# Moments of x1 by an accumulator and a ScalarE pass of squares; the last chunk of A h0 in two groups between the maps

## The chip, the cores and the metric

One core of one Trainium2 chip runs the whole program. The metric is the device time of one execution in microseconds (us). The engines are TensorE (PE, with its weight loads PEld), VectorE (DVE), ScalarE (ACT), GpSimd (POOL) and SyncE (SP, which here only issues DMAs). Each engine works through its own instructions in order and waits at semaphores.

## The reference, cut to what matters

Two graph layers over 1250 nodes with 512 features and 40000 edges.

```python
h0 = relu(layernorm(x))
msg = (h0[src] + edge_attr) @ Wm.T + bm                       # first layer
agg = segment_sum(msg, dst) / max(deg, 1)
out = h0 + gelu(concat(h0, agg) @ Wu.T + bu)
x1  = x + layernorm(out) * gamma + beta
h1  = relu(layernorm(x1))                                     # second layer
rst = (1 + eps) * h1 + segment_sum(h1[src], dst)
x2  = x1 + relu(rst @ W1 + b1) @ W2 + b2 + h1
```

## The kernel before, in words

Nodes lie in NT = 10 blocks of 128. A is the 1250 x 1250 matrix of edge counts, so that a sum over neighbours is a product with A. Up to about 251 us the kernel streams the edges, builds A and forms most of A h0. What is left of A h0 is the chunk of the last 226 nodes: ten `piece` steps on PE, each with eight matmuls, called in groups by `late` (L1292) between the maps.

The change lies in the stretch that follows, from 251 to about 331 us, in which the first layer ends and the second begins. Its order is written out by hand, one loop for each engine, with k as the step and b as the block:

- PE (L1296 to L1319): `map_agg(b)` multiplies block b's sums with the folded weights; `late` puts the ten pieces behind maps 2, 3, 4 and 5 as groups of 2, 3, 3 and 2; from b = 5 on `transpose_h1(b - 5)` and from b = 6 on `times_A(b - 6, "A")` follow each map, and after map 9 there are only transposes, `times_A` of chunk A and of chunk B as a filler. `map_agg(b)` waits for `update(b - 2)` of DVE, because it writes into the same PSUM bank. `transpose_h1(b)` waits for `h1(b)` of ACT.
- DVE (L997 to L1005): the list `STEPS` gives each piece of work with a lag; in step k it does `update(k)`, `center(k-2)`, `add_h0(k-1)`, `add_x(k-2)`, `o_moments(k-1)`, `shift(k-3)`, `x1_moments(k-2)`, `add_beta(k-1)`, `o_moments2(k-1)`, `x1_moments2(k-2)`, `o_variance(k-1)`, `x1_variance(k-2)` and `low_h1(k-4)`. `add_x(b)` writes x1 of block b to `U`; `x1_moments` and `x1_moments2` take its mean and variance with the two batch-norm instructions.
- ACT (L591 to L598): in step k a conversion `full_conv(k + 2)` of A, `gelu(k)`, `h0_again(k + 1)`, then `h1(k-3)`, `h1_high(k-3)` and `h1T(k-3)`. `h0_again(b)` makes h0 of a block again from a fresh copy of x in one of three buffers `xt`, and waits until that copy has landed.
- SP (`load_x`, L370): the copy of x for block b goes into `xt[b % 3]`, so from b = 3 on SP waits for `add_x(b - 3)`, the last reader of that buffer, before it issues the DMA.
- POOL (L429 to L436): the two powers of -1/2, `rs` for the first layer norm and `rs2` for that of x1.

`shift(b)` makes the bias of `h1(b)` from `rs2`, and `low_h1(b)` the low part of h1 that `times_A(b)` needs.

Of the kernel before, what the change touches and what calls it, by code (L numbers as in the profile page):

```python
# [5 lines left out]
F32 = mybir.dt.float32  # L6
# [4 lines left out]
ALU = mybir.AluOpType  # L11
# [3 lines left out]
P = 128  # L15
# [7 lines left out]
EPS = 1e-5  # L23
# [7 lines left out]
def gnn_kernel(nc, x, src, dst, edge, Wm, bm, Wu, bu, gamma, beta, W1, b1, W2, b2, eps, out):  # L31
# [54 lines left out]
    assert IN_LOOP <= 2 * NT and HAS_AT[-1] < NG and DEG_AT < OUT_AT and len(FOLD_AT) == HB - 1  # L86
    assert len(BIAS_AT) == NT and all(BIAS_AT[b] <= HAS_AT[b] for b in range(NT))
    DEG_BANK = 2
    CHUNK_BANK = [0, 1, 4, 5]

    at = [-(-nc.sbuf_base // 64) * 64]

    def place(name, shape, dt, offset=None):
        size = mybir.dt.size(dt)
        for n in shape[1:]:
            size *= n
        if offset is None:
            offset = at[0]
            at[0] += -(-size // 32) * 32
        return nc.alloc_sbuf_tensor_at(name, shape, dt, offset=offset), offset  # L100
# [91 lines left out]
    rs0, _ = place("rs0", [P, NT], F32)  # L192
    nb0, _ = place("nb0", [P, NT], F32)
    nb, _ = place("nb", [P, NT], F32)
    degs, _ = place("degs", [P, NT], F32)
    rdeg, _ = place("rdeg", [P, NT], F32)
    has, _ = place("has", [P, NT], F32)
    assert at[0] <= nc.sbuf_usable_end, at[0] - nc.sbuf_usable_end
# [2 lines left out]
    with ctx:  # L201
        ps = ctx.enter_context(nc.psum_tensor("ps", [P, 8, 512], F32))

        def sem(name):
            return ctx.enter_context(nc.semaphore(name))
# [95 lines left out]
        wu2_in = [sem(f"wu2_in{half}") for half in range(2)]  # L301
        wuT_done = sem("wuT_done")
        wuT_mm = sem("wuT_mm")
        x1_aggr = sem("x1_aggr")
        x1_ready = sem("x1_ready")
        x1_stats = sem("x1_stats")
        x_in = sem("x_in")
        xb_ready = sem("xb_ready")
        y_done = sem("y_done")
# [81 lines left out]
        @block.gpsimd  # L391
        def _(pool):
            nc.gpsimd.memset(dst_i[:], NP - 1).then_inc(pads_set, 1)
            nc.gpsimd.memset(src_i[:], 0).then_inc(pads_set, 1)
            nc.gpsimd.iota(iotaF[:], [[1, P]], base=0, channel_multiplier=0, allow_small_or_imprecise_dtypes=True).then_inc(consts, 1)
            nc.gpsimd.iota(pid[:], [[1, 1]], base=0, channel_multiplier=1, allow_small_or_imprecise_dtypes=True).then_inc(consts, 1)
            nc.gpsimd.memset(mhalf[:], -0.5).then_inc(consts, 1)
            nc.gpsimd.memset(onesF[:], 1.0).then_inc(consts, 1)
            nc.gpsimd.memset(offs[:], 0).then_inc(consts, 1)
            nc.gpsimd.memset(X[:, NT - 1, :], 0.0).then_inc(pads_set, 1)  # L400
            nc.gpsimd.iota(iotaP[:], [[1, 256], [0, 2]], base=0, channel_multiplier=0, allow_small_or_imprecise_dtypes=True).then_inc(consts, 1)

            pool.wait_ge(bm_in, 16)
            nc.gpsimd.tensor_copy(bmB[:], bmC[:].rearrange("p (m a) -> p m a", a=1).broadcast_to([P, FC, P])).then_inc(bmB_done, 1)

            pool.wait_ge(consts, 3)
            pool.wait_ge(ve_ready, 1)
            nc.gpsimd.tensor_tensor(rs0[:], ve[:], mhalf[:], ALU.pow).then_inc(rs_ready, 1)

            def add_sums_of(n):  # L410
                _, loaded = nc.values_load_multi_w_load_instructions(
                    offrow[0:1, n * 4:n * 4 + 2].bitcast(I32), engines=(mybir.EngineType.Pool,), min_val=0, max_val=(NP << 16) - 1,
                    skip_runtime_bounds_check_because="a pair of least indices of nodes")
                for half, first in enumerate((loaded[0] & 0xFFFF, loaded[0] >> 16)):
                    first = nc.s_assert_within(first, 0, NP - 1, skip_runtime_bounds_check_because="each is the least of indices of nodes")
                    cols = aggT[:, :, bass.ds(first, W)]
                    if half == 0:
                        pool.wait_ge(turned_out, n + 1)
                    if n > 0 or half > 0:
                        pool.wait_ge(early_step, n * 2 + half)  # L420
                    sums = turned_sums[n % TURNS][:].rearrange("p (f q) -> p f q", f=FC)[:, :, half * QUAD:half * QUAD + W]
                    nc.gpsimd.tensor_tensor(cols, sums, cols, ALU.add).then_inc(early_step, 1)  # L422

            pool.wait_ge(offs_in, 16)
            pool.wait_ge(sums_zero, 1)
            for n in range(EARLY):
                add_sums_of(n)

            for k in range(NT + 1):  # L429
                if k < NT:  # L430
                    pool.wait_ge(ve1_ready, k + 1)
                    nc.gpsimd.tensor_tensor(rs[:, k:k + 1], ve[:, k:k + 1], mhalf[:, 0:1], ALU.pow).then_inc(rs1_ready, 1)  # L432
                if k > 0:
                    b = k - 1
                    pool.wait_ge(ve2_ready, b + 1)
                    nc.gpsimd.tensor_tensor(rs2[:, b:b + 1], ve2[:, b:b + 1], mhalf[:, 0:1], ALU.pow).then_inc(rs2_ready, 1)  # L436

            pool.wait_ge(h1_ready, NT)
            pool.wait_ge(split1, NT)
            with pool.Fori(0, NT) as b:  # L440
                t = U[:, bass.ds(b, 1), :]
                nc.gpsimd.tensor_tensor(t, t, b2B[:].rearrange("p (a d) -> p a d", a=1), ALU.add).then_inc(res_step, 1)
                pool.wait_ge(res_step, b * 3 + 1)
                nc.gpsimd.tensor_tensor(t, t, Hh[:, bass.ds(b, 1), :].bitcast(F32), ALU.add).then_inc(res_step, 1)
                pool.wait_ge(res_step, b * 3 + 2)
                nc.gpsimd.tensor_tensor(t, t, Hl[:, bass.ds(b, 1), :].bitcast(F32), ALU.add).then_inc(res_step, 1)
# [3 lines left out]
        def _(act):  # L450
# [108 lines left out]
            def full_conv(c):  # L559
                nc.scalar.copy(AR[:, c, :], A16[:, c, 0:NP]).then_inc(conv, 1)  # L560
# [7 lines left out]
            def gelu(b):  # L568
                act.wait_ge(t_ready, b + 1)
                nc.scalar.activation(tt[b % TB][:], tt[b % TB][:], ACT.Gelu).then_inc(g_ready, 1)  # L570

            def h1(b):
                act.wait_ge(nb2_ready, b + 1)
                act.wait_ge(piece_mm, 2 * NT + b + 1)
                nc.scalar.activation(X[:, b, :], U[:, b, :], ACT.Relu, bias=nb[:, b:b + 1], scale=rs2[:, b:b + 1]).then_inc(h1_ready, 1)

            def h1_high(b):
# [9 lines left out]
            act.wait_ge(eps_ready, 2)  # L587
            full_conv(0)
            h0_again(0)
            full_conv(1)  # L590
            for k in range(NT + 4):  # L591
                if k + 2 < NT:
                    full_conv(k + 2)
                for work, lag in ((gelu, 0), (h1, 3), (h1_high, 3), (h1T, 3)):
                    if 0 <= k - lag < NT:
                        work(k - lag)
                    if work is gelu and k + 1 < NT:
                        h0_again(k + 1)  # L598
# [15 lines left out]
        def _(dve):  # L614
# [352 lines left out]
            def add_x(b):  # L967
                dve.wait_ge(centered, b + 1)
                dve.wait_ge(rs1_ready, b + 1)
                dve.wait_ge(xb_ready, b + 1)  # L970
                V.scalar_tensor_tensor(U[:, b, :], tt[b % TB][:], rs[:, b:b + 1], xt[b % TB][:], ALU.mult, ALU.add).then_inc(x1_ready, 1)

            def x1_moments(b):
                dve.wait_ge(x1_ready, b + 1)
                V.bn_stats(stats[:, b, :], U[:, b, :]).then_inc(x1_stats, 1)

            def x1_moments2(b):
                dve.wait_ge(x1_stats, b + 1)
                V.bn_aggr(mv2[:, b, :], stats[:, b, :]).then_inc(x1_aggr, 1)

            def x1_variance(b):
                dve.wait_ge(x1_aggr, b + 1)
                V.tensor_scalar(ve2[:, b:b + 1], mv2[:, b, 1:2], EPS, None, ALU.add).then_inc(ve2_ready, 1)

            def shift(b):
                dve.wait_ge(rs2_ready, b + 1)
                V.scalar_tensor_tensor(nb[:, b:b + 1], mv2[:, b, 0:1], -1.0, rs2[:, b:b + 1], ALU.mult, ALU.mult).then_inc(nb2_ready, 1)

            def low_h1(b):
                dve.wait_ge(hi1_ready, b + 1)  # L990
# [3 lines left out]
            dve.wait_ge(late_in, 48)  # L994
            dve.wait_ge(deg_step, 3 + NT)

            STEPS = [(update, 0), (center, 2), (add_h0, 1), (add_x, 2), (o_moments, 1), (shift, 3), (x1_moments, 2), (add_beta, 1), (o_moments2, 1),  # L997
                     (x1_moments2, 2), (o_variance, 1), (x1_variance, 2), (low_h1, 4)]
            for k in range(NT + 5):
                if k == 5:  # L1000
                    dve.wait_ge(piece_mm, 3 * NT)
# [27 lines left out]
        def _(pe):  # L1029
# [262 lines left out]
            def late(count):  # L1292
                for _ in range(count):
                    piece(late_pieces.pop(0))

            for b in range(5):  # L1296
                map_agg(b)
                late((0, 0, 2, 3, 3)[b])
            for b in range(5, NT):
                map_agg(b)  # L1300
                if b == 5:
                    late(2)
                    assert not late_pieces
                transpose_h1(b - 5)
                if b == 6:
                    pe.wait_ge(agg_done, 2 * FC + 1)
                if b > 5:
                    times_A(b - 6, "A")
# [74 lines left out]
```

## Time and profile before

| | us |
|---|---|
| median of 3 runs (489.90 to 492.35) | 490.38 |
| the profiled execution | 489.93 |
| its span | 488.1 |
| PE busy | 472.6 (97%) |
| DVE busy | 269.4 (55%) |
| ACT busy | 158.0 (32%) |
| POOL busy | 122.2 (25%) |

The profile is of one execution. The span runs from the first to the last instruction; 1.83 us of the execution's time lie outside it. In a timeline row the first number is the start in us from the span's start, the second the duration, then engine, line, operation, output and inputs, and in brackets the idle time before the row with what ended it. Instructions overlap by about 0.1 us on ACT and DVE, so what one costs its engine is read from start to start. The modelled end of a matmul lies up to 0.17 us behind the start of the next one.

### The profile page before, as it was taken

To read this page: it belongs to the slowest core of one execution; us is meant where nothing else is said; L and a number is where in the kernel's file an instruction comes from. 1 tells how busy PE (TensorE), PEld (TensorE's weight loads), DVE (VectorE), ACT (ScalarE), POOL (GpSimd) and SP (SyncE) were. 2 spreads that over 40 slices of the span, in tenths; PEclk is the share of its full clock that TensorE was granted. 3 is DMA by queue.
4 is the path that set the end of the run, shared out by engine and by line. 5 is a ranking of instruction groups with operands and counts; after the bars stand their busy time and mean duration, and the time that the engine had idled before them with its cause. 6 is when DMAs were issued, how large, how long until landed. Compare 5 with 4: busy or idle time off the path is not lost.

```text
span 488.1 us, 9290 instructions
## 1 busy us (share of the span) xinstructions
PE 472.6 (97%) x3275; PEld 277.4 (57%) x3275; DVE 269.4 (55%) x621; ACT 158.0 (32%) x291; POOL 122.2 (25%) x183
## 2 busy tenths in 40 slices
PE   4999999999999999999999999899999999999997
PEld 3545555555555446776766655699744449444442
DVE  4789878787878887977857699923000000011011
ACT  6726633332333327411047287620012123000000
POOL 4005433444343432000001113349990000000000
PEclk9899999999999999999999999999999999999999
DMA  8998999999999999999430111040130000010111
GB/s 297 381 351 282 410 389 395 398 407 401 396 391 397 397 401 405 401 339 299 147 109 24 43 30 53 0 173 1 45 128 1 0 0 1 21 43 21 44 43 38
DMA packets 31641, 98.92 MB, mean 203 GB/s; under 512 B 3593, under 2 KB 4617, under 8 KB 31595
## 3 DMA queue, kind: packets, MB, share of 16 engines
q1 hardware_dynamic: 30458, 97.27, 53.1%
q10 hardware_dynamic: 1136, 1.05, 0.7%
q8 instruction: 27, 0.44, 0.4%
q14 instruction: 20, 0.16, 0.1%
HBM read 95.76 MB, written 2.56 MB: 201 GB/s over the span
## 4 chain that ended last, share of the span: by engine, by line
PE 81%; DVE 10%; DMA 4%; issue 3%; SPq 1%; POOL 1%; DVEq 0%; POOLq 0%
PE ps L1355 14%; PE ps L1340 14%; PE ps L1091 10%; PE ps L1137 7%; PE ps L1110 6%; PE ps L1190 6%; PE ps L1191 5%; PE ps L1287 4%; PE ps L1099 4%; DMA X<-in_x_dram 4%; PE ps L1119 4%; PE ps L1263 3%; PE ps L1264 3%; DVE A L696 2%; DVE stats L777 1%
## 5 line engine op out<-in xcount | busy, mean ns | idle before, releaser
L422 POOL TENSOR_TENSOR aggT<-turned_sums,aggT 128x88 f32 x118 | 62.5, 530 | 88.1 <-ACT turned_sums L487 74.8
L1025 DVE TENSOR_TENSOR U<-ps,U 128x512 f32<-128x512 f32 (+1 forms) x10 | 6.9, 693 | 128.5 <-PE ps L1355 128.5
L696 DVE TENSOR_TENSOR A<-ps,A 128x220 f32 x158 | 60.7, 384 | 28.6 <-PE ps L1110 18.0
L1355 PE MATMUL ps<-W2s,hid 128*128 128x512 f32 (+1 forms) x160 | 68.8, 592 | 0.0
L1340 PE MATMUL ps<-aggT,W1s 128*128 (+1 forms) x192 | 67.3, 513 | 0.0
L1091 PE MATMUL ps<-ea,oneD 128*22 128x256 f32 x944 | 62.7, 383 | 0.0
L1340 PEld LDWEIGHTS ps<-aggT,W1s 128*128 128x128 f32 x192 | 36.4, 190 | 30.7 <-issue 30.6
L1355 PEld LDWEIGHTS ps<-W2s,hid 128*128 128x128 f32 (+1 forms) x160 | 30.0, 188 | 38.2 <-issue 38.2
L481 ACT COPY packed_sums<-ps 128x256 f32<-128x256 f32 x59 | 22.0, 372 | 90.4 <-PE ps L1091 90.4
L1091 PEld LDWEIGHTS ps<-ea,oneD 128*22 128x22 f32 x944 | 22.6, 101 | 46.5 <-issue 21.7
L1263 PE MATMUL ps<-AR,Hh 128*128 128x256 f32 (+2 forms) x160 | 44.0, 311 | 0.7 <-DVE Hl L992 0.7
L1264 PE MATMUL ps<-AR,Hl 128*128 128x256 f32 (+2 forms) x160 | 43.0, 306 | 0.0
L1110 PE MATMUL ps<-oneK,oneS 128*128 128x220 bf16 x316 | 41.2, 260 | 1.7 <-DVE A L696 1.5
L675 DVE TENSOR_TENSOR oneK<-iotaP,P_key 128x1760 bf16<-128x1760 bf16 (+1 forms) x40 | 42.3, 1057 | 0.0
L1137 PE MATMUL ps<-Wu1T,U 128*128 128x512 f32 x80 | 41.3, 598 | 0.0
L605 ACT ACTIVATE hid<-ps,b1C 128x512 f32 (+1 forms) x24 | 14.6, 608 | 77.7 <-PE ps L1340 77.7
L432 POOL TENSOR_TENSOR rs<-ve,mhalf 128x1 f32<-128x1 f32 x10 | 8.3, 829 | 113.1 <-DVE ve L957 113.1
L1287 PE MATMUL ps<-CT,aggT 128*128 128x512 f32 x80 | 35.7, 592 | 0.0
L1190 PE MATMUL ps<-ARc,Hh 128*128 128x512 f32 x80 | 33.8, 423 | 0.0
L1110 PEld LDWEIGHTS ps<-oneK,oneS 128*128 128x128 bf16 x316 | 29.7, 97 | 5.0 <-DVE oneK L675 2.2
L1263 PEld LDWEIGHTS ps<-AR,Hh 128*128 128x128 f32 x160 | 30.2, 189 | 2.7 <-DVE Hl L992 1.1
L1191 PE MATMUL ps<-ARc,Hl 128*128 128x512 f32 x80 | 31.6, 394 | 0.0
(133 smaller groups left out, 642.7 us busy)
## 6 DMA issues: line engine op xcount, KB each, us to landing
ea<-in_edge_attr_dram SPq DMA_DIRECT2D x78, 1024.0 KB, 7.8
X<-in_x_dram SPq DMA_DIRECT2D x1, 2304.0 KB
xt<-in_x_dram SPq DMA_DIRECT2D x9, 256.0 KB, 3.5
out_dram<-U SPq DMA_DIRECT2D x9, 256.0 KB
W1s<-in_L_gnn_W_dram SPq DMA_DIRECT2D x1, 2048.0 KB, 9.1
W2s<-in_L_gnn_W_dram SPq DMA_DIRECT2D x1, 2048.0 KB, 8.5
WuN<-in_L_gnn_Wu_dram ACTq DMA_DIRECT2D x2, 512.0 KB, 4.4
WuN<-in_L_gnn_Wu_dram SPq DMA_DIRECT2D x1, 1024.0 KB, 6.8
```

The lines of the kernel that those rows point to most:

```text
L422: nc.gpsimd.tensor_tensor(cols, sums, cols, ALU.add).then_inc(early_step, 1)
L696: V.tensor_tensor(cols, ps[:, 4 + m % 2, half * KW:(half + 1) * KW].rearrange("p (h w) -> p h w", w=W), cols, ALU.add).then_inc(add_step, 1)
L1091: last = T.matmul(to.rearrange("p (c d) -> p c d", c=2), oneD[h][:, g * 2 + j, :], data, start=j == 0, stop=j == 1)
L1110: last = T.matmul(ps[:, 4 + m % 2, (j // 2) * KW:(j // 2 + 1) * KW], sources[:, j // 2, :, j % 2], keys[:, j // 2, :, j % 2], start=j % 2 ...
L1137: quarter = T.matmul(ps[:, ASIDE_BANK["u1", b], :], U[:, b, f * P:(f + 1) * P], Wu1T[:, f, :], start=f == 0, stop=f == FC - 1)
L1190: T.matmul(to, Hh[:, c, rows], here, start=c == 0 and (q < 2 or f % 2 == 0), stop=False)
L1191: last = T.matmul(to, Hl[:, c, rows], here, start=False, stop=c == NT - 1 and (q < 2 or f % 2 == 1))
L1263: T.matmul(to, Hh[:, b, rows], AR[:, b, start:start + cols], start=b == 0 and (cols == 512 or f % 2 == 0), stop=False)
L1264: last = T.matmul(to, Hl[:, b, rows], AR[:, b, start:start + cols], start=False, stop=b == NT - 1 and (cols == 512 or f % 2 == 1))
L1287: last = T.matmul(ps[:, 2 + b % 2, :], aggT[:, f, b * P:(b + 1) * P], CT[:, f, :], start=f == 0, stop=f == FC - 1)
L1340: last = T.matmul(ps[:, CHUNK_BANK[k % 4], 0:cols], W1s[:, f, k * P:(k + 1) * P], aggT[:, f, bass.ds(start, cols)], start=f == 0, stop=f = ...
L1355: last = T.matmul(ps[0:rows, 6 + b % 2, :], hid[:, k, b * P:b * P + rows], W2s[:, k, :], start=k == 0, stop=k == KC - 1)
```

## The change

The two batch-norm instructions on x1 are replaced. `add_x` also writes the sum of its output row into `x1_sum` (laid over `degs`, which is no longer read by then). `x1_moments` becomes one [128 x 1] multiplication that makes minus the mean. A new ACT step `x1_squares` squares `U` plus that bias into `X` (which `h1` overwrites afterwards) and accumulates the sum of squares. `x1_variance` on DVE waits for that and moves from lag 2 near the end of a step to lag 3 at its head; `shift` moves behind `x1_moments`. On ACT `x1_squares(k-2)` stands behind `gelu(k)` and `h0_again(k+1)` and ahead of `h1(k-3)`. Two more conversions of A run before the ACT loop, whose own conversions begin at k = 2. POOL's loop takes `rs2(k-2)` ahead of `rs(k)`. On PE the ten pieces stand in two groups of five, behind map 1 and map 3.

```diff
+    CONV_AHEAD = 4
+    degs, degs_at = place("degs", [P, NT], F32)
+    x1_sum, _ = place("x1_sum", [P, NT], F32, degs_at)
...
-            for k in range(NT + 1):
+            for k in range(NT + 2):
+                if k >= 2:
+                    b = k - 2
+                    pool.wait_ge(ve2_ready, b + 1)
+                    nc.gpsimd.tensor_tensor(rs2[:, b:b + 1], ve2[:, b:b + 1], mhalf[:, 0:1], ALU.pow).then_inc(rs2_ready, 1)
                 if k < NT:
                     pool.wait_ge(ve1_ready, k + 1)
...
-                if k > 0:
-                    b = k - 1
-                    pool.wait_ge(ve2_ready, b + 1)
...
+            def x1_squares(b):
+                act.wait_ge(x1_mean, b + 1)
+                act.wait_ge(piece_mm, 2 * NT + b + 1)
+                nc.scalar.activation(X[:, b, :], U[:, b, :], ACT.Square, bias=mv2[:, b, 0:1], accum_out=mv2[:, b, 1:2]).then_inc(x1_square, 1)
...
-            full_conv(1)
+            for c in range(1, CONV_AHEAD):
+                full_conv(c)
             for k in range(NT + 4):
-                if k + 2 < NT:
-                    full_conv(k + 2)
-                for work, lag in ((gelu, 0), (h1, 3), (h1_high, 3), (h1T, 3)):
+                if k >= 2 and k - 2 + CONV_AHEAD < NT:
+                    full_conv(k - 2 + CONV_AHEAD)
+                for work, lag in ((gelu, 0), (x1_squares, 2), (h1, 3), (h1_high, 3), (h1T, 3)):
                     if 0 <= k - lag < NT:
                         work(k - lag)
                     if work is gelu and k + 1 < NT:
...
-                V.scalar_tensor_tensor(U[:, b, :], tt[b % TB][:], rs[:, b:b + 1], xt[b % TB][:], ALU.mult, ALU.add).then_inc(x1_ready, 1)
+                V.scalar_tensor_tensor(U[:, b, :], tt[b % TB][:], rs[:, b:b + 1], xt[b % TB][:], ALU.mult, ALU.add,
+                                       accum_out=x1_sum[:, b:b + 1]).then_inc(x1_ready, 1)
...
-                V.bn_stats(stats[:, b, :], U[:, b, :]).then_inc(x1_stats, 1)
-
-            def x1_moments2(b):
-                dve.wait_ge(x1_stats, b + 1)
-                V.bn_aggr(mv2[:, b, :], stats[:, b, :]).then_inc(x1_aggr, 1)
+                V.tensor_scalar(mv2[:, b, 0:1], x1_sum[:, b:b + 1], -1.0 / D, None, ALU.mult).then_inc(x1_mean, 1)
 
             def x1_variance(b):
-                dve.wait_ge(x1_aggr, b + 1)
-                V.tensor_scalar(ve2[:, b:b + 1], mv2[:, b, 1:2], EPS, None, ALU.add).then_inc(ve2_ready, 1)
+                dve.wait_ge(x1_square, b + 1)
+                V.tensor_scalar(ve2[:, b:b + 1], mv2[:, b, 1:2], 1.0 / D, EPS, ALU.mult, ALU.add).then_inc(ve2_ready, 1)
...
-            STEPS = [(update, 0), (center, 2), (add_h0, 1), (add_x, 2), (o_moments, 1), (shift, 3), (x1_moments, 2), (add_beta, 1), (o_moments2, 1),
-                     (x1_moments2, 2), (o_variance, 1), (x1_variance, 2), (low_h1, 4)]
+            STEPS = [(x1_variance, 3), (update, 0), (center, 2), (add_h0, 1), (add_x, 2), (o_moments, 1), (x1_moments, 2), (shift, 3), (add_beta, 1),
+                     (o_moments2, 1), (o_variance, 1), (low_h1, 4)]
...
-                late((0, 0, 2, 3, 3)[b])
+                late((0, 5, 0, 5, 0)[b])
...
-                if b == 5:
-                    late(2)
-                    assert not late_pieces
                 transpose_h1(b - 5)
```

## Rows read from the trace of the kernel before

**Rows 1.** Stretches: length, busy PE, PEld, DVE, ACT, POOL, granted clock, DMA share, GB/s.

```profile
12.00:14.00 2.00, 2.00 (x8) 1.41 (x7) 1.86 (x5) 1.17 (x2) 0.00 (x0) 0.50 1.01 403
280.00:325.00 45.00, 42.32 (x200) 29.67 (x199) 38.12 (x89) 30.52 (x43) 10.78 (x14) 1.00 0.21 69
290.00:305.00 15.00, 14.64 (x54) 8.80 (x53) 15.00 (x38) 10.91 (x17) 3.96 (x5) 1.00 0.18 50
```

**Rows 2.** Timeline of DVE, its step k = 8.

```profile
299.22 0.75 DVE L940 SCALAR_TENSOR_TENSOR tt<-ps,rdeg,U 128x512 f32<-128x512 f32 x1
...
300.54 0.68 DVE L945 TENSOR_TENSOR tt<-tt,h0t 128x512 f32<-128x512 f32 x1
301.14 0.74 DVE L971 SCALAR_TENSOR_TENSOR U<-tt,rs,xt 128x512 f32<-128x512 f32 x1
...
302.47 0.68 DVE L975 BATCH_NORM_STATS2 stats<-U 128x6 f32<-128x512 f32 x1
...
303.95 0.15 DVE L983 TENSOR_SCALAR ve<-mv 128x1 f32<-128x1 f32 x1
304.02 0.69 DVE L992 TENSOR_TENSOR Hl<-X,Hh 128x512 fp32r<-128x512 f32 x1
304.63 0.74 DVE L940 SCALAR_TENSOR_TENSOR tt<-ps,rdeg,U 128x512 f32<-128x512 f32 x1
```

**Rows 3.** Timeline of PE, maps 7 and 8, transposes of h1 of blocks 5 and 9.

```profile
287.51 3.60 PE L1287 MATMUL ps<-CT,aggT 128*128 128x512 f32 x8
...
293.25 3.60 PE L1287 MATMUL ps<-CT,aggT 128*128 128x512 f32 x8
...
306.35 0.63 PE L1272 MATMUL ps<-ident,X 128*128 128x128 f32 x4 [0.88 <-issue]
...
322.91 0.60 PE L1272 MATMUL ps<-ident,X 128*128 128x128 f32 x4
```

**Rows 4.** Timeline of PE, maps 0 to 4; last two rows DVE's, update(2), low_h1(0).

```profile
251.15 10.47 PE L1287 MATMUL ps<-CT,aggT 128*128 128x512 f32 x24
...
263.23 3.60 PE L1287 MATMUL ps<-CT,aggT 128*128 128x512 f32 x8
...
269.34 3.60 PE L1287 MATMUL ps<-CT,aggT 128*128 128x512 f32 x8
...
261.65 0.75 DVE L940 SCALAR_TENSOR_TENSOR tt<-ps,rdeg,U 128x512 f32<-128x512 f32 x1
...
281.39 0.69 DVE L992 TENSOR_TENSOR Hl<-X,Hh 128x512 fp32r<-128x512 f32 x1 [3.52 <-PE ps L1272]
```

**Rows 5.** Timelines of DVE and ACT: add_x (L971), h0_again (L566), h1 (L575).

```profile
263.58 0.74 DVE L971 SCALAR_TENSOR_TENSOR U<-tt,rs,xt 128x512 f32<-128x512 f32 x1
267.11 0.82 ACT L566 ACTIVATE h0t<-xt,nb,rs 128x512 f32<-128x512 f32 x1 [3.12 <-DMA xt<-in_x_dram]
...
268.80 0.75 DVE L971 SCALAR_TENSOR_TENSOR U<-tt,rs,xt 128x512 f32<-128x512 f32 x1
272.05 0.81 ACT L566 ACTIVATE h0t<-xt,nb,rs 128x512 f32<-128x512 f32 x1 [2.44 <-DMA xt<-in_x_dram]
272.77 0.80 ACT L575 ACTIVATE X<-U,nb,rs 128x512 f32<-128x512 f32 x1
...
290.33 0.74 DVE L971 SCALAR_TENSOR_TENSOR U<-tt,rs,xt 128x512 f32<-128x512 f32 x1
295.63 0.81 ACT L566 ACTIVATE h0t<-xt,nb,rs 128x512 f32<-128x512 f32 x1 [1.68 <-DMA xt<-in_x_dram]
```

**Rows 6.** Groups of ACT by line and shape: busy us, mean ns | idle before.

```profile
L566 ACT ACTIVATE h0t<-xt,nb,rs 128x512 f32<-128x512 f32 x10 | 8.1, 808 | 7.5 <-DMA xt<-in_x_dram 7.5
...
L570 ACT ACTIVATE tt<-tt 128x512 f32<-128x512 f32 x10 | 6.3, 626 | 0.0
...
L546 ACT ACT_TABLE_LOAD x1 | 1.3, 1283 | 0.0
L546 ACT ACTIVATE warm<-onesF 128x1 f32<-128x1 f32 x1 | 0.2, 203 | 0.0
```

More of the change, by code:

```diff
@@ L194, in gnn_kernel @@
     nb, _ = place("nb", [P, NT], F32)
-    degs, _ = place("degs", [P, NT], F32)
+    degs, degs_at = place("degs", [P, NT], F32)
+    x1_sum, _ = place("x1_sum", [P, NT], F32, degs_at)
     rdeg, _ = place("rdeg", [P, NT], F32)
@@ L303, in gnn_kernel @@
         wuT_mm = sem("wuT_mm")
-        x1_aggr = sem("x1_aggr")
+        x1_mean = sem("x1_mean")
         x1_ready = sem("x1_ready")
-        x1_stats = sem("x1_stats")
+        x1_square = sem("x1_square")
         x_in = sem("x_in")
@@ L432, in _ @@
                     nc.gpsimd.tensor_tensor(rs[:, k:k + 1], ve[:, k:k + 1], mhalf[:, 0:1], ALU.pow).then_inc(rs1_ready, 1)
-                if k > 0:
-                    b = k - 1
-                    pool.wait_ge(ve2_ready, b + 1)
-                    nc.gpsimd.tensor_tensor(rs2[:, b:b + 1], ve2[:, b:b + 1], mhalf[:, 0:1], ALU.pow).then_inc(rs2_ready, 1)
             pool.wait_ge(h1_ready, NT)
@@ L570, in gelu @@
                 nc.scalar.activation(tt[b % TB][:], tt[b % TB][:], ACT.Gelu).then_inc(g_ready, 1)
+            def x1_squares(b):
+                act.wait_ge(x1_mean, b + 1)
+                act.wait_ge(piece_mm, 2 * NT + b + 1)
+                nc.scalar.activation(X[:, b, :], U[:, b, :], ACT.Square, bias=mv2[:, b, 0:1], accum_out=mv2[:, b, 1:2]).then_inc(x1_square, 1)
             def h1(b):
                 act.wait_ge(nb2_ready, b + 1)
-                act.wait_ge(piece_mm, 2 * NT + b + 1)
+                act.wait_ge(x1_square, b + 1)
                 nc.scalar.activation(X[:, b, :], U[:, b, :], ACT.Relu, bias=nb[:, b:b + 1], scale=rs2[:, b:b + 1]).then_inc(h1_ready, 1)
@@ L970, in add_x @@
                 dve.wait_ge(xb_ready, b + 1)
-                V.scalar_tensor_tensor(U[:, b, :], tt[b % TB][:], rs[:, b:b + 1], xt[b % TB][:], ALU.mult, ALU.add).then_inc(x1_ready, 1)
+                V.scalar_tensor_tensor(U[:, b, :], tt[b % TB][:], rs[:, b:b + 1], xt[b % TB][:], ALU.mult, ALU.add,
+                                       accum_out=x1_sum[:, b:b + 1]).then_inc(x1_ready, 1)
             def x1_moments(b):
                 dve.wait_ge(x1_ready, b + 1)
-                V.bn_stats(stats[:, b, :], U[:, b, :]).then_inc(x1_stats, 1)
-            def x1_moments2(b):
-                dve.wait_ge(x1_stats, b + 1)
-                V.bn_aggr(mv2[:, b, :], stats[:, b, :]).then_inc(x1_aggr, 1)
+                V.tensor_scalar(mv2[:, b, 0:1], x1_sum[:, b:b + 1], -1.0 / D, None, ALU.mult).then_inc(x1_mean, 1)
             def x1_variance(b):
-                dve.wait_ge(x1_aggr, b + 1)
-                V.tensor_scalar(ve2[:, b:b + 1], mv2[:, b, 1:2], EPS, None, ALU.add).then_inc(ve2_ready, 1)
+                dve.wait_ge(x1_square, b + 1)
+                V.tensor_scalar(ve2[:, b:b + 1], mv2[:, b, 1:2], 1.0 / D, EPS, ALU.mult, ALU.add).then_inc(ve2_ready, 1)
             def shift(b):
                 dve.wait_ge(rs2_ready, b + 1)
-                V.scalar_tensor_tensor(nb[:, b:b + 1], mv2[:, b, 0:1], -1.0, rs2[:, b:b + 1], ALU.mult, ALU.mult).then_inc(nb2_ready, 1)
+                V.tensor_tensor(nb[:, b:b + 1], mv2[:, b, 0:1], rs2[:, b:b + 1], ALU.mult).then_inc(nb2_ready, 1)
             def low_h1(b):
```

## The prediction

> **What bounds the kernel now.** I read the stretches first, then DVE's and ACT's timelines between 251 and 331 us, then PE's. PE is the bound of the whole, and the stretch that the change touches is no exception: from 280 to 325 us PE is busy 42.32 of 45 us [rows 1], so it waits for 2.68 us in all. Those waits, and up to about 1 us more that the modelled ends of the matmuls before them hide, are all that a shorter DVE could give back. Inside that stretch DVE sets the pace: from 290 to 305 us it is busy 15.00 of 15.00 us, ACT 10.91 [rows 1]. One DVE step lasts 299.22 to 304.63 = 5.41 us [rows 2]. What PE does in a step there (a map, the transposes of a block, a block of chunk A) is 287.51 to 293.25 = 5.74 us with no wait inside [rows 3]. So DVE and PE run almost in step, and PE's waits stand at the transposes, as before block 5 at 306.35 [rows 3].
>
> **What the change takes off DVE.** Each step loses the batch-norm statistics of x1, 0.61 us from start to start with 0.68 busy [rows 2], and a small aggregate; it gains a [128 x 1] multiplication, about 0.07 by x1_variance's 303.95 to 304.02 [rows 2]. That alone would make the DVE step some 4.9 us, under PE's. How much of it counts depends on the new order of waits.
>
> **The new wait.** x1_variance(b) now stands at the head of DVE's step b+3 and waits for x1_squares(b) of ACT's step b+2. Behind that wait in DVE's queue stand update, center, add_h0 and add_x, the whole step. On ACT x1_squares(b) stands behind h0_again(b+3), which waits for the copy of x of block b+3 to land. SP issues that copy only once add_x(b) has released the buffer. So there is a closed round: x1_variance(b), update(b+3), center(b+1), add_h0(b+2), add_x(b+1), load of block b+4, h0_again(b+4), x1_squares(b+1), x1_variance(b+1). Before, the same late load only made ACT wait (7.5 us in four places [rows 6]); DVE did not ask ACT for anything that lay behind it until a step later.
>
> **One round, from rows.** x1_variance to the next instruction 0.07; update and center 299.22 to 300.54, 1.32; add_h0 300.54 to 301.14, 0.60; add_x 0.74 to its end [rows 2]. Then the load: from add_x's end to h0_again's start it took 267.11 - 264.32 = 2.79, 272.05 - 269.55 = 2.50 and once 295.63 - 291.07 = 4.56 us [rows 5]. Seven blocks load this way; I take the mean of the two near ones, 2.65, and one slow load in seven, (4.56 - 2.65) / 7 = 0.27: 2.9. h0_again to the next ACT instruction 272.05 to 272.77 = 0.72 [rows 5].
>
> Two prices have no row. **x1_squares:** gelu, with no pointer operand, takes 0.626 and h0_again, with two, 0.808 [rows 6]; with its one I take 0.72. Writing out the accumulator may be a further small instruction: nothing at least, 0.40 at most (two of the 128 x 1 activation of 0.203 [rows 6]); I take one, 0.20, since that is the smallest ACT instruction there is. Together 0.92, bounds 0.63 and 1.21. **The accumulator of add_x:** nothing at least, 0.20 at most in the plain case; I take 0.07, the issue of a [128 x 1] DVE instruction [rows 2]. Below nothing is excluded for both: the instructions do all that they did before, or are new.
>
> Sum: 0.07 + 1.32 + 0.60 + 0.81 + 2.9 + 0.72 + 0.92 = 7.34 us a round, against 5.41 on DVE and 5.74 on PE. ACT's own work does not reach that: 10.91 / 15 x 5.41 = 3.9 a step plus 0.92.
>
> A rule of the Trainium skill speaks against the accumulator: Vector Engine (DVE) Microarchitecture Reference, section "Points that are easy to get wrong", says that a scalar-tensor-tensor with two SBUF sources that are not bf16 runs at half throughput. add_x is one such already, without an accumulator, and takes 0.74 against add_h0's 0.68 [rows 2], so the trace does not show it; by the page each round would be longer, which is a rival below.
>
> **The two groups of pieces.** On PE nothing is won or lost by grouping: a map is 3.43 (three end after 10.47 and one lasts 3.60, so (10.47 - 3.60) / 2), a map and three pieces take 263.23 to 269.34 = 6.11 [rows 4], so a piece costs (6.11 - 3.43) / 3 = 0.89 with its change of weights in it. But all five of the first group now stand ahead of map 2, where none stood. update(2) waits for map 2, so it moves from 261.65 [rows 4] by 5 x 0.89 = 4.47 to 266.12. In the kernel before, DVE had room for that: it waited 3.52 us at low_h1(0), 281.39 [rows 4]. Now the rounds start there.
>
> **The other moves.** The two conversions ahead of the ACT loop cost nothing: ACT then waits for update(2) and the first load, as it did for 3.12 us before 267.11 [rows 5]. POOL's new order puts rs2 first, as DVE asks for it; shift has five DVE instructions of cover behind x1_variance. SP's queue: the load of W1, behind the last copy of x, waits for the last add_x and moves with it; what needs it moves as well. POOL's residual adds, which wait for the last h1, do the same.
>
> **The sum.** update(2) at 266.12; add_x(0) ends 1.32 + 0.60 + 0.81 = 2.73 later, 268.85; load, 271.75; h0_again, 272.47; x1_squares(0) done at 273.39. Six rounds of 7.34, 44.04, bring x1_squares(6) to 317.43; it is the last that stands behind a load (block 9). h1(5) follows on ACT, 0.80 [rows 5], and its transpose starts at 318.3 with a handover of 0.1. Before it started at 306.35 [rows 3]: 12.0 later. From there to the transpose of block 9 took 16.56 [rows 3], nearly all PE's work; it stays, give or take 0.5. PE's waits inside the rounds (7.34 - 5.74 = 1.6 each, and a long one where map 9 is done and update(9) is not) are this same time seen from PE, not a further cost. So the profiled execution goes from 489.93 to 501.9. The median of the runs lies 0.45 above that execution; 490.38 + 12.0 = **502.4**.
>
> Low end: load 2.50, squares 0.63, no price for add_x: 6.58 a round, 0.76 less in seven passes (the first pass and six rounds), -5.3: 497.1. High end: load 2.79 with two slow ones of seven, 3.30, squares 1.21, add_x 0.20: 8.16 a round, +0.82 x 7 = 5.7: 508.1.
>
> **Rivals.**
> - *DVE's gain counts (faster).* If x1_squares never waited behind a load, the pace would be PE's 5.74, and PE's waits of 2.68 and the 1 hidden behind modelled ends would go: 486.7. It decides where the round falls under 5.74: all terms but the load make 4.44, so the load must take under 1.3 us from add_x's end. The shortest in the trace is 2.50. For it: the chain of work that DVE carries is truly shorter, and one DVE-bound stretch is the only one with PE waits. 0.05.
> - *The load is hidden, but so is the gain (same).* With the load covered, update(2) still comes 4.47 late against a room of 3.52 [rows 4], about 1 us lost at the first transposes, and the rest a draw: 491.4. 0.07.
> - *The accumulating add_x passes at half rate (slower still).* Its issue, 0.66 by the update and center before it, doubles; some 0.6 x 7 = 4.2 more: 506.6. DVE is then not relieved at all, and the change does not do what it says. Against it is add_x's 0.74 today. 0.08.
> - *Square needs another table than Gelu.* Table loads are two in the whole trace, of 1.283 each, the last ahead of the first Gelu [rows 6], though Copy, Relu and Gelu alternate; if Square were not in the same table, x1_squares would carry one inside the round and gelu one outside: at least 1.28 x 7 = 9 more, 511. The Trainium skill, ScalarE: Activation LUTs, section "Table sets: the hidden batching unit", names relu, copy, identity and abs as present in every set and does not name square there; by its price of about 2.7 us for a switch (an estimate from that page) it would be some 19 more. 0.03.
> - *The clock.* PE runs at 1.00 throughout this stretch; early in the trace it was granted 0.50 at 12 to 14 us [rows 1], behind PE's idle start. With waits of 1.6 in each round and some 5 us before the transpose of block 5 it may fall again; at half rate a stretch like that one costs 1 to 3 us beyond what the rounds' own room covers: 503 to 505. 0.07.
>
> **How the numbers follow.** The forecast has 0.70, the rivals what stands behind them. The range is 497 to 508: it takes in the bounds of the unknown costs, the clock and the half rate, and leaves out the two cases without a loss, the table loads and a little at both ends, some 2 in 10. A measurement of this kernel can tell about 0.5% (2.5 us) from no change. Faster 0.05, same 0.07, slower 0.88.
>
> **What would show it.** Right: in the timeline of DVE after, x1_variance idles about 2.3 us in each of steps 4 to 9 and its releaser is ACT's Square; ACT's h0_again idles before almost each block, released by the DMA; the distance between two x1_variance is 7 to 7.5; the transpose of block 5 starts near 318, and all that follows keeps its length. Wrong: h0_again without idle time, DVE steps near 5, or PE without waits between 285 and 318. Accumulator and squares are read off directly: 0.74 to 0.81 for add_x, 0.7 to 0.9 for Square with its read. What would make it wrong altogether is a load that lands a good deal sooner than 2.5 us after add_x.

## The result and the profile after

The changed kernel takes 499.99 us (median of 5 runs, 499.79 to 502.46) against 490.38 for the kernel before: a ratio of 1.0189, 95% interval 1.0163 to 1.0214, 9.6 us slower. The forecast was 502.4, in a range of 497 to 508.

The profiled execution of the changed kernel took 502.46 us, the longest of its five; 2.87 us of what it has over that of before lie ahead of the first map (254.02 in place of 251.15 [rows 4]), where the two programs are the same. About half of this came up between 190 and 222 us, a stretch in which the granted clock fell to 0.50 for some 3 us and that of before did not. The stretch in question is therefore compared from its own first map on. From there to the transpose of block 9 it was 322.91 - 251.15 = 71.76 us before [rows 3, 4]; after it is 335.47 - 254.02 = 81.45, that is 9.69 more, as much as the medians lie apart. The timeline of PE after, first map and the transposes of blocks 1, 5, 6 and 9:

```profile
254.02 7.03 PE L1292 MATMUL ps<-CT,aggT 128*128 128x512 f32 x16
...
290.36 0.66 PE L1277 MATMUL ps<-ident,X 128*128 128x128 f32 x4 [2.77 <-ACT X L582]
...
318.16 1.11 PE L1277 MATMUL ps<-ident,X 128*128 128x128 f32 x4 [4.40 <-DVE tt L948]
323.99 0.60 PE L1277 MATMUL ps<-ident,X 128*128 128x128 f32 x4
...
335.47 0.60 PE L1277 MATMUL ps<-ident,X 128*128 128x128 f32 x4
```

PE now waits 2.77 us for block 1 and 4.40 us for block 5, where the row of before has 0.88 [rows 3]. The wait at block 5 ends with update(9): in both programs PE waits for the last update once, ahead of the transposes of blocks 5 to 9 (`pe.wait_ge(t_ready, NT)`). What lies behind it stands in the chain of work that ended last, here from one load of x to the next (start, duration, what):

```profile
278.63 2.57 DMA xt<-in_x_dram
281.36 0.58 issue
281.94 0.81 ACT X L577 x2
282.94 0.56 issue
283.50 0.74 DVE tt L969
284.25 0.60 DVE tt L953
284.84 0.68 DVE U L979 x2
285.55 2.51 DMA xt<-in_x_dram
```

This is the closed round, link by link: the load, h0_again (in the first "issue" piece), x1_squares on ACT (L577), x1_variance and update (in and just ahead of the second "issue" piece), center (L969), add_h0 (L953), add_x (L979), and the next load, which that add_x released. The chain repeats it seven times, and the load is its largest piece. The same round on DVE and on ACT, one step of each:

```profile
275.85 0.15 DVE L988 TENSOR_SCALAR ve<-mv 128x1 f32<-128x1 f32 x1 [2.65 <-ACT X L577]
275.92 0.74 DVE L948 SCALAR_TENSOR_TENSOR tt<-ps,rdeg,U 128x512 f32<-128x512 f32 x1
...
277.85 0.75 DVE L979 SCALAR_TENSOR_TENSOR U<-tt,rs,xt 128x512 f32<-128x512 f32 x1
278.52 0.08 DVE L979 DVE_READ_ACCUMULATOR U<-tt,rs,xt 128x1 f32 x1
278.52 0.69 DVE L957 BATCH_NORM_STATS2 stats<-tt 128x6 f32<-128x512 f32 x1
...
282.77 0.15 DVE L988 TENSOR_SCALAR ve<-mv 128x1 f32<-128x1 f32 x1 [2.57 <-ACT X L577]
...
317.29 0.15 DVE L988 TENSOR_SCALAR ve<-mv 128x1 f32<-128x1 f32 x1 [1.81 <-ACT X L577]
317.36 0.74 DVE L948 SCALAR_TENSOR_TENSOR tt<-ps,rdeg,U 128x512 f32<-128x512 f32 x1
```

```profile
281.22 0.81 ACT L568 ACTIVATE h0t<-xt,nb,rs 128x512 f32<-128x512 f32 x1 [3.72 <-DMA xt<-in_x_dram]
281.94 0.71 ACT L577 ACTIVATE X<-U,mv 128x512 f32<-128x512 f32 x1
282.55 0.19 ACT L577 ACTIVATION_READ_ACCUMULATOR X<-U,mv 128x1 f32 x1
...
317.17 0.80 ACT L582 ACTIVATE X<-U,nb,rs 128x512 f32<-128x512 f32 x1
```

x1_variance (L988) waits 2.65 and 2.57 us at the head of its step, for ACT; ACT's h0_again has just waited 3.72 for the load. The last row of each is update(9) and h1(5) (L582). Six rounds last 317.29 - 275.85 = 41.44 us, 6.91 each, against a step of 5.41 before [rows 2].

### The profile page after: what moved, and what is told of

It reads as the page before. It is cut to its first block, busy times and chain, and to the rows that moved or that the text cites. A ratio compares the mean times of both kernels' runs of the same rounds, so it can differ in the third digit from the quotient of the medians.

```text
span 500.7 us, 9320 instructions
## 1 busy us (share of the span) xinstructions
PE 476.4 (95%) x3275; PEld 280.2 (56%) x3275; DVE 264.0 (53%) x621; ACT 165.4 (33%) x311; POOL 121.5 (24%) x183
## 4 chain that ended last, share of the span: by engine, by line
PE 78%; DMA 7%; DVE 7%; issue 4%; ACT 1%; SPq 1%; DVEq 1%; POOL 0%; ACTq 0%; POOLq 0%
PE ps L1357 14%; PE ps L1342 13%; PE ps L1096 10%; PE ps L1142 7%; PE ps L1115 5%; PE ps L1195 5%; PE ps L1196 4%; PE ps L1268 4%; PE ps L1269 4%; DMA X<-in_x_dram 4%; PE ps L1104 4%; DMA xt<-in_x_dram 4%; PE ps L1124 4%; PE ps L1292 2%; DVE A L704 2%
## 5 line engine op out<-in xcount | busy, mean ns | idle before, releaser
L1268 PE MATMUL ps<-AR,Hh 128*128 128x256 f32 (+2 forms) x160 | 45.4, 319 | 0.0
L1269 PE MATMUL ps<-AR,Hl 128*128 128x256 f32 (+2 forms) x160 | 44.4, 313 | 0.0
L1268 PEld LDWEIGHTS ps<-AR,Hh 128*128 128x128 f32 x160 | 31.3, 196 | 1.8
```

The costliest lines, as they stand in the source:

```text
L1268: T.matmul(to, Hh[:, b, rows], AR[:, b, start:start + cols], start=b == 0 and (cols == 512 or f % 2 == 0), stop=False)
L1269: last = T.matmul(to, Hl[:, b, rows], AR[:, b, start:start + cols], start=False, stop=b == NT - 1 and (cols == 512 or f % 2 == 1))
```

## The experiments

All are compared with the kernel before on the same chip; the ratio is the kernel's time over that of the kernel before. "Transpose 5" and "stretch" are read from the one profile of each run, in us: from the first map to the transpose of block 5, and to that of block 9. The theory: the round through the load sets the pace. The rivals: the ScalarE pass and DVE's wait for it cost the time whatever stands ahead of them; the two groups of pieces cost it; the clock does.

| kernel | ratio, 95% interval | transpose 5 | stretch |
|---|---|---|---|
| before | | 55.20 | 71.76 |
| changed | 1.0189 (1.0163 to 1.0214) | 64.14 | 81.45 |
| squares ahead of h0_again | 1.0017 (0.9995 to 1.0040) | 56.81 | 72.40 |
| four buffers for x | 1.0042 (1.0027 to 1.0058) | 56.44 | 73.13 |
| wait behind add_x | 0.9977 (0.9956 to 0.9999) | 56.03 | 70.92 |
| four groups again | 1.0132 (1.0098 to 1.0166) | 62.52 | 79.20 |
| groups alone, on before | 1.0025 (1.0010 to 1.0040) | 55.63 | 72.62 |
| load in four parts | 1.0285 (1.0266 to 1.0304) | 68.10 | 85.58 |
| PE kept busy | 1.0192 (1.0173 to 1.0211) | 63.98 | 80.67 |
| open round | 0.9942 (0.9927 to 0.9957) | 53.54 | 68.82 |
| its order alone, on before | 1.0025 (1.0006 to 1.0044) | 55.63 | 72.07 |
| open round, two groups | 0.9951 (0.9933 to 0.9969) | 53.55 | 68.82 |

**The squares ahead of the load.** One line of ACT's order in the changed kernel:

```diff
-                    if work is gelu and k + 1 < NT:
+                    if work is x1_squares and k + 1 < NT:
                         h0_again(k + 1)
```

> The changed kernel with one edit: on ACT x1_squares(k-2) runs ahead of h0_again(k+1) instead of behind it, so no load stands between add_x(b) and x1_squares(b). Theory (the closed round through the load sets the pace, 6.91 us in the profile after): x1_variance to x1_variance falls to PE's 5.7, PE loses only its first transposes, and the time is 491 to 492 us. Rival 1 (the added pass on ACT and the wait of DVE for it cost the time, whatever stands ahead): the pass still lies on the way to h1 and DVE still waits for it at the head of its step, so the time stays at 498 to 500. Rival 2 (the two groups of pieces cost it): stays at 500.

Measured: 492.01 us, ratio 1.0017. The groups of ACT and DVE in its stretch (busy us, mean ns | idle before):

```profile
L568 ACT ACTIVATE h0t<-xt,nb,rs 128x512 f32<-128x512 f32 x10 | 8.1, 810 | 3.4 <-DMA xt<-in_x_dram 3.4
L988 DVE TENSOR_SCALAR ve<-mv 128x1 f32<-128x1 f32 x10 | 1.5, 151 | 3.2 <-ACT X L577 3.1
```

In the changed kernel the same two groups read:

```profile
L568 ACT ACTIVATE h0t<-xt,nb,rs 128x512 f32<-128x512 f32 x10 | 8.1, 810 | 16.6 <-DMA xt<-in_x_dram 16.6
L988 DVE TENSOR_SCALAR ve<-mv 128x1 f32<-128x1 f32 x10 | 1.5, 153 | 14.3 <-ACT X L577 14.3
```

x1_variance waits 3.2 us in all where the changed kernel has 14.3, with the same pass on ACT and the same wait at the head of DVE's step. Of the 9.69 us in the stretch, 9.05 are gone.

**The load a round earlier.** A fourth buffer, with all orders kept:

```diff
+    XB = 4
-    xt = [... w1_at + i * 2048)[0] for i in range(TB)]
+    xt = [... w1_at + i * 2048)[0] for i in range(XB)]
...
-                if b >= TB:
-                    sp.wait_ge(x1_ready, b - TB + 1)
+                if b >= XB:
+                    sp.wait_ge(x1_ready, b - XB + 1)
...
```

> The changed kernel with four buffers for the copies of x instead of three (the fourth lies in room that is free by then), all orders as in the changed kernel: the load for block b waits for add_x(b-4) instead of add_x(b-3), so it is issued one round earlier. Theory: h0_again no longer waits for a landing, the round loses the 2.6 us of the load and PE's 5.7 sets the pace; 491.5 to 492.5 us, a little over the kernel with the squares ahead, since h0_again's 0.72 stays in the round. Rival 1 (the added ACT pass and DVE's wait): 498 to 500. Rival 2 (groups): 500.

Measured: 492.91 us, ratio 1.0042. In the groups of ACT the wait for the load is gone, and it was the load alone that was moved; x1_variance still waits 3.8 us in all, for the pass on ACT:

```profile
L569 ACT ACTIVATE h0t<-xt,nb,rs 128x512 f32<-128x512 f32 x10 | 8.1, 806 | 0.0
L989 DVE TENSOR_SCALAR ve<-mv 128x1 f32<-128x1 f32 x10 | 1.5, 152 | 3.8 <-ACT X L578 3.8
```

**The wait elsewhere in DVE's queue.** `(x1_variance, 3)` behind `(add_x, 2)`, `(shift, 3)` behind `(add_beta, 1)`:

```diff
-            STEPS = [(x1_variance, 3), (update, 0), (center, 2), (add_h0, 1), (add_x, 2), (o_moments, 1), (x1_moments, 2), (shift, 3), (add_beta, 1),
+            STEPS = [(update, 0), (center, 2), (add_h0, 1), (add_x, 2), (x1_variance, 3), (o_moments, 1), (x1_moments, 2), (add_beta, 1), (shift, 3),
...
```

> The changed kernel with x1_variance moved in DVE's step from the head to behind add_x (shift goes behind add_beta); ACT's order, the buffers and the groups stay. Theory: what is wrong is what is queued behind the wait: add_x(b+1) no longer waits for x1_squares(b), so the load of block b+4 is released early and the round is open although each load still stands ahead of its squares; 489 to 491 us. Rival 1 (the pass itself is what costs): x1_squares ends no earlier against its add_x than now, 4.2 us behind it, and h1 waits for it as now, so 497 to 500.

Measured: 490.56 us, ratio 0.9977, so not slower than before at all. Each load still stands ahead of its squares; what changed is that add_x no longer queues behind the wait:

```profile
L988 DVE TENSOR_SCALAR ve<-mv 128x1 f32<-128x1 f32 x10 | 1.5, 152 | 0.1
L568 ACT ACTIVATE h0t<-xt,nb,rs 128x512 f32<-128x512 f32 x10 | 8.1, 806 | 4.8 <-DMA xt<-in_x_dram 4.8
```

So three different links, each opened by itself, give back nearly all. The first rival would have kept 497 us or more in each; it falls.

**More load.** The same bytes as four DMAs of 32 rows:

```diff
-                sp.dma_start(xt[b % TB][0:rows, :], x[b * P:b * P + rows, :]).then_inc(xt_in[b % TB], 16)
+                for n in range(4):
+                    part = slice(n * 32, min(rows, n * 32 + 32))
+                    sp.dma_start(xt[b % TB][part, :], x[b * P + part.start:b * P + part.stop, :]).then_inc(xt_in[b % TB], 16)
...
-                act.wait_ge(xt_in[b % TB], 16 * (b // TB + 1))
+                act.wait_ge(xt_in[b % TB], 64 * (b // TB + 1))
```

> The changed kernel with each load of x issued as four DMAs of 32 rows in place of one: same bytes, but the last is issued about 3 x 0.33 = 1 us later on SP's queue. Theory (every load lies in the round, in seven passes): each wait of h0_again ends about 1 us later, round 7.9 in place of 6.9, and the time grows by some 7 us, to 505 to 508. Rival 1 (the ACT pass, not the load, sets the round): the same 500 as the changed kernel, since ACT idles 1.5 us ahead of h0_again anyway.

Measured: 504.92 us, ratio 1.0285, just under what was expected, because a load came later by 0.6 and not by 1 us: h0_again starts 3.28 us behind the end of add_x in its third step, 274.12 - 270.84, where the changed kernel has 2.65 (274.30 - 271.65). Seven loads by 0.6 make 4.2; the stretch is 85.58 - 81.45 = 4.13 longer. Both engines of the round, ACT and DVE, have idle time in every step of this kernel, and still every 0.6 us of load is paid in full.

```profile
270.09 0.75 DVE L981 SCALAR_TENSOR_TENSOR U<-tt,rs,xt 128x512 f32<-128x512 f32 x1
...
274.12 0.81 ACT L570 ACTIVATE h0t<-xt,nb,rs 128x512 f32<-128x512 f32 x1 [4.54 <-DMA xt<-in_x_dram]
281.58 0.81 ACT L570 ACTIVATE h0t<-xt,nb,rs 128x512 f32<-128x512 f32 x1 [4.27 <-DMA xt<-in_x_dram]
```

**The groups.** First the changed kernel with `late((0, 0, 2, 3, 3)[b])` and `late(2)` behind map 5 again:

> The changed kernel with the ten pieces back in their four groups (2, 3, 3, 2 behind maps 2 to 5); the new moments stay. Theory: the rounds start earlier by at most the 4.47 us that map 2 no longer waits, less what PE's own first transpose, which cannot come sooner, holds them up: 1.5 to 2.5 us faster than the changed kernel, 497.5 to 498.5. Rival 2 (the groups are what costs): 490 to 491.

Measured: 497.79 us, ratio 1.0132; the stretch 2.25 us shorter than the changed kernel's. Then the kernel before with `late((0, 5, 0, 5, 0)[b])` alone:

> The kernel before with only the regrouping of the ten pieces (five behind map 1, five behind map 3); moments by the batch-norm instructions as before. Theory: on PE the grouping itself is free; DVE starts its steps 4.47 us later at update(2) and has 3.5 us of room, so about 0.9 us is lost at the transpose of block 1 and not won back: ratio 1.002 (491.3 us). Rival (the groups carry a good part of the loss): 494 or more. If the old version was right to have no room elsewhere, below 490.

Measured: ratio 1.0025, the stretch 0.86 longer, as large as expected but not where it was expected. Block 1's transpose lies 34.00 us behind the first map, as before (33.99); it is update(5) that starts 286.27 - 253.54 = 32.73 behind it where it was 283.01 - 251.15 = 31.86, and DVE, with steps of 5.4 us, carries these 0.87 us on until PE waits for update(9), ahead of the transpose of block 5:

```profile
286.27 0.74 DVE L940 SCALAR_TENSOR_TENSOR tt<-ps,rdeg,U 128x512 f32<-128x512 f32 x1
...
309.17 0.63 PE L1272 MATMUL ps<-ident,X 128*128 128x128 f32 x4 [1.89 <-DVE tt L940]
```

Of the 0.86 us, 0.43 stand at that transpose (55.63 against 55.20 in the table). The other 0.43 lie behind it, where the granted clock also fell, to 0.66 on average from 310 to 315 us; how much of this half is the clock's is open. So the groups cost up to 0.9 us by themselves, and 2.25 beside the closed round, whose start they delay. They are not what cost the 9.6.

**The clock.** In the changed kernel the granted clock falls at the 4.40 us wait: in stretches of half a microsecond it is 0.50, the lower of its two levels (1.2 and 2.4 GHz), from 317.0 to 323.5 us. In stretches of 5 us (length, PE busy, granted clock, DMA share, GB/s):

```profile
315.00:320.00 5.00, 1.84 (x7) 0.69 0.03 11
320.00:325.00 5.00, 5.00 (x22) 0.63 0.00 0
```

The edit puts matmuls into that wait, whose results the next transposes overwrite:

```diff
+    DUMMY = 16
...
+            pe.wait_ge(h1T_done, 4)
+            for n in range(DUMMY):
+                T.matmul(ps[:, 7, :], Hh[:, 0, 0:P], AR[:, 0, 0:512], start=n == 0, stop=n == DUMMY - 1)
             pe.wait_ge(t_ready, NT)
```

> The changed kernel with 16 extra matmuls of 128 x 512 on PE where it waits some 4.4 us for update(9) (their results are overwritten by the transposes that follow). In the profile after, PE's granted clock is 0.69 and 0.63 in the 10 us behind that wait, and the transposes of blocks 5 and 6 lie 5.83 us apart against 3.24 before. Theory: the clock falls because of that idle time; with PE kept busy it stays at 1.00, the two transposes lie 4.3 apart as the rounds of DVE and ACT ask, and the time is 0.5 to 1.5 us under the changed kernel's 500, the rest being hidden. Rival: the extra matmuls come on top and the time is 500 or more, the clock the same.

Measured: 500.35 us, ratio 1.0192, no different from the changed kernel's: the gain of 0.5 to 1.5 us that was expected did not show. Where it was meant to, the clock stayed at 1.00 in the one execution that was profiled, and the transposes of blocks 5 and 6 lie 321.82 - 317.68 = 4.14 us apart in place of 5.83. But in this execution it fell elsewhere, behind the wait for block 1, and without cost there, since the rounds have room:

```profile
290.00:295.00 5.00, 4.87 (x13) 0.50 0.17 52
...
320.00:325.00 5.00, 4.30 (x29) 1.00 0.00 0
```

Between the transposes of blocks 5 and 9 this kernel takes 334.37 - 317.68 = 16.69 us, the changed one 17.31, the kernel before 16.56 [rows 3]. The kernel with four buffers, whose clock stayed at 1.00 there, takes 16.69 as well (73.13 - 56.44). So the clock's fall costs about 0.6 us of the changed kernel's stretch, an estimate from one execution of each, and too little to be seen in the times of this run.

**A version that opens the round.** In DVE's step x1_variance stands behind center, shift behind add_x, low_h1 behind o_moments; ACT's order is gelu, h1, x1_squares, h1_high, h0_again, h1T; four groups.

```diff
-            STEPS = [(x1_variance, 3), (update, 0), (center, 2), (add_h0, 1), ...
+            STEPS = [(update, 0), (center, 2), (x1_variance, 3), (add_h0, 1), (add_x, 2), (shift, 3), (o_moments, 1), (low_h1, 4), (x1_moments, 2),
+                     (o_moments2, 1), (add_beta, 1), (o_variance, 1)]
...
-                for work, lag in ((gelu, 0), (x1_squares, 2), (h1, 3), (h1_high, 3), (h1T, 3)):
+                for work, lag in ((gelu, 0), (h1, 3), (x1_squares, 2), (h1_high, 3), (h1T, 3)):
...
-                    if work is gelu and k + 1 < NT:
+                    if work is h1_high and k + 1 < NT:
...
```

> The changed kernel's moments (accumulator and ScalarE pass) in an order with no closed round: in DVE's step x1_variance behind center, shift behind add_x, low_h1 behind o_moments; on ACT gelu, h1, x1_squares, h1_high, h0_again, h1T; the four old groups of pieces. Theory: PE's waits between blocks 1 and 5 go (0.6, 0.5 and 1.05 us), and with the later ones in part too: 2 to 2.8 us of the 3.6 that PE lost there, ratio 0.994 to 0.996 against the kernel before (487.8 to 488.5). Rival 1 (the pass on ACT costs time of its own): no better than the kernel before, 490 or more.

Measured: 487.67 us, ratio 0.9942 (0.9927 to 0.9957): faster than both kernels, by 2.9 us against before on the same chip (490.55). DVE's step is 4.9 us, and PE's wait for update(9) shrinks to 0.45:

```profile
288.98 0.74 DVE L948 SCALAR_TENSOR_TENSOR tt<-ps,rdeg,U 128x512 f32<-128x512 f32 x1
...
293.87 0.74 DVE L948 SCALAR_TENSOR_TENSOR tt<-ps,rdeg,U 128x512 f32<-128x512 f32 x1
...
305.13 0.66 PE L1277 MATMUL ps<-ident,X 128*128 128x128 f32 x4 [0.45 <-DVE tt L948]
```

Whether the order or the moments won this was asked with the same order in the kernel before (h0_again behind h1_high, shift behind add_x, low_h1 behind o_moments; batch-norm moments as before):

> The kernel before, its moments by the batch-norm instructions and its four groups kept, with only the order of the open-round version: in DVE's step shift behind add_x, low_h1 behind o_moments, and on ACT h0_again behind h1_high. Theory: what the open-round version won (ratio 0.9942) is the DVE time that the new moments free; with the batch-norm instructions DVE's step stays 5.4 us and the order alone wins nothing: 490 to 491.5 us, ratio 0.999 to 1.003. Rival: the order was the gain, and the moments did nothing: 487.5 to 488.5, ratio 0.994 to 0.996.

Measured: ratio 1.0025; the order alone wins nothing, and the interval lies above 1. Its steps on DVE are still 5.37 us (290.29 to 295.66), and PE waits 2.54 us for update(9):

```profile
290.29 0.74 DVE L940 SCALAR_TENSOR_TENSOR tt<-ps,rdeg,U 128x512 f32<-128x512 f32 x1
...
295.66 0.74 DVE L940 SCALAR_TENSOR_TENSOR tt<-ps,rdeg,U 128x512 f32<-128x512 f32 x1
...
307.19 0.66 PE L1272 MATMUL ps<-ident,X 128*128 128x128 f32 x4 [2.54 <-DVE tt L940]
```

Last, the open round with the two groups of five:

> The open-round version with the two groups of five in place of the four. Theory: the 0.9 us that the groups cost the kernel before came of DVE's small room behind a later update(2); with a DVE step near 4.9 us the room is there, and the groups cost nothing: 487.5 to 488.5 us, ratio 0.994 to 0.996, the same as with four groups. Rival: the groups cost their 0.9 us (ratio 1.0025 alone) whatever DVE does: 488.5 to 489.5, ratio 0.9965.

Measured: ratio 0.9951, and a stretch of 68.82, the same to the hundredth as with four groups. The interval alone (0.9933 to 0.9969) would not exclude the rival's 0.9965; the equal stretches speak for the theory, that a DVE with room pays nothing for a later update(2).

## Why the prediction was right

- **What bounds.** Right. PE's waits in the stretch were the ceiling of a gain: the open round took 2.94 us off the stretch (71.76 to 68.82), of the 2.68 and about 1 more that the prediction counted. DVE's step is 4.89 us there, where the prediction had some 4.9.
- **The new wait and the round.** Right in every link of the round; the chain of work names them in the order in which the prediction did. The link behind it was another: PE's transpose of block 5 was released by update(9), which ended at 318.10, and not by h1(5), which had ended at 317.97. Both come straight behind x1_squares(6), 0.13 us apart, so the sum hardly changes.
- **The signs.** h0_again waits for the DMA ahead of all seven blocks. x1_variance waits 2.65, 2.57, 0.88, 1.93, 2.21, 1.83 and 1.81 us for x1_squares, mean 1.98 in place of about 2.3, and two of them lie 6.91 apart on average and not 7 to 7.5. That the transpose of block 5 started at 318.16, "near 318", and that the profiled execution took 502.46 where 501.9 was forecast, is luck: this execution reached its first map 2.87 us later than that of before. Counted from there the transpose came at 64.14 and not at 318.3 - 251.15 = 67.15.
- **The size of the round.** 7.34 was forecast, 6.91 came. The load was the term taken too large: from add_x's end to h0_again it took 2.65, 2.62, 2.57, 2.62, 2.89, 2.51 and 2.49 us, mean 2.62 against 2.9. No load of this execution was as slow as the one of 4.56 before [rows 5], which the prediction had spread over seven. x1_squares took 275.85 - 275.02 = 0.83 to DVE's start (0.92 forecast), and add_x with its accumulator 0.75 (0.81). 0.28 + 0.09 + 0.06 = 0.43 a round.
- **The start.** update(2) 14.96 us behind the first map, 14.97 forecast, by five pieces at 0.89.
- **The sum.** The transpose of block 5 came 8.94 us later against the first map, 12.0 forecast: seven passes of 0.43. From there to block 9 the prediction gave 0 with 0.5 either way; it was 17.31 against 16.56, 0.75 more, of which the clock makes about 0.6 by the estimate above. It offset a part of what the rounds had been given too much. 8.94 + 0.75 = 9.69.
- **The half rate** that the Trainium skill names (Vector Engine (DVE) Microarchitecture Reference, "Points that are easy to get wrong") fell: add_x with two f32 sources in SBUF and an accumulator takes 0.747 us on average, without one 0.745, and update, which has one of its sources in PSUM, takes 0.74 too. What the skill says of the accumulator, that it is written out by an instruction of its own (VectorE: DVE Perf Modes, "Two Vector instructions with no wait between them"), the trace agrees with: the read is a row, 0.08 us, and hidden, since the next instruction starts beside it at 278.52.
- **The table loads** fell: there are two, as before, so in this kernel Square and Gelu need no load between them.
- **The clock** fell at the long wait that the prediction named, though not at those inside the rounds, and cost less than the 1 to 3 us given, about 0.6. The earlier fall, which the prediction put behind PE's idle start, did not follow it at once: in the kernel before PE's first matmul starts at 4.65 us, and the clock fell between 11.0 and 11.5 us, with another wait of 1.68 us ahead of 10.02 in between.
- **DVE's gain** was real: the rival that counted on it failed only by the round, as the open version shows (ratio 0.9942). A shorter load was not needed for that: with the wait behind add_x a load of x still takes 2.6 us (median) from issue to landing, against 2.5 in the changed kernel, but no longer lies in the round.
- **The load hidden, and the gain with it.** The fourth buffer makes this rival's case: it gave 491.4 us, and 492.91 came.

## What to carry to other kernels

Ahead of moving work to an engine with time to spare, follow the new wait once around: what is queued behind the waiting instruction, what that releases, and what stands ahead of the awaited one in its own queue. If a transfer lies on that path, its whole latency is paid in every step, however idle the engines look: here 2.6 of 6.9 us a round. Opening any one link (a buffer more, the wait further back in the queue, the awaited work ahead of the other engine's wait) was enough here to come back to about the time of before (ratios 0.9977 to 1.0042). The saved work itself counted clearly only when both queues were put in an order in which little waits (0.9942).

## What was not expected of the hardware

TensorE's granted clock fell from 1.00 to 0.50, that is from 2.4 to 1.2 GHz, for 3 to 7 us in several of these stretches, and the length of the wait just before does not tell when. It fell at waits of 4.40 us (changed kernel), 2.54 (order alone) and 1.89 (groups alone), yet stayed at 1.00 behind 3.44 (load in four parts, block 1), 2.77 (changed kernel, block 1) and 2.36 (squares ahead). At the wait for block 1 it fell with PE kept busy (2.85) and not in the changed kernel (2.77), whose program is the same up to there. In the profiled execution of the changed kernel it also fell to 0.50 from 218 to 221 us, though no wait of PE is recorded from 195 to 222 us. What decides it stays open.
